# VectorE reads a unit's values before the expert sum, the next unit's maximum and the GRU's products

## What is computed

```python
x = x + attn(lstm(x, cond, Wx, Wh, b), Wq, Wkv_down, Wk_up, Wv_up, Wout)
x = x + moe(gru(x, cond, Wz, bz, Wr, br, Wh, bh, Wp, bp), gate_w, w1, b1, w2, b2)

# lstm, for each of 128 steps
a = xW[t] + h @ Wh;  i, f, o = sigmoid(a[:, :384]);  g = tanh(a[:, 384:])
c = f * c + i * g;   h = o * tanh(c)
# attn: 16 heads of 64, keys and values from a latent of 32, causal, softmax over 128 keys
# gru, for each of 128 steps
z = sigmoid([x_t, h] @ Wz + bz);  r = sigmoid([x_t, h] @ Wr + br)
h_new = (1 - z) * h + z * tanh([x_t, r * h] @ Wh + bh)
h = tanh(h_new @ Wp + bp) if (t + 1) % 4 == 0 and t < 127 else h_new
# moe: 8 experts 128 -> 512 -> 128 with gelu, the best 2 of a softmax gate
```

## Time and profile before

| | |
|---|---|
| median of 3 runs | 856.5 us (852.35 to 860.57) |
| profiled execution, its own time | 853.5 us |
| its span | 851.6 us |
| mean granted TensorE clock | 0.836 of full |
| busy: TensorE, VectorE, ScalarE, GpSimd | 80%, 47%, 42%, 15% |

### The profile page before, as it was taken

One profiled execution on the slowest core, in us unless ns is written; L12 is line 12 of the kernel. 1 busy time (PEld: TensorE's weight loads), 2 busy tenths in 40 slices (PEclk: granted clock), 3 DMA queues, 4 the chain that ended last, 5 costly groups with the idle time before them and its releaser, 6 DMA issues.

```text
span 851.6 us, 19294 instructions
## 1 busy us (share of the span) xinstructions
PE 679.1 (80%) x7090; PEld 603.3 (71%) x7090; DVE 398.2 (47%) x2308; ACT 354.2 (42%) x1240; POOL 131.5 (15%) x339
## 2 busy tenths in 40 slices
PE   6968978877788777887788778887888787788888
PEld 3536756777678667776777677776877677777787
DVE  2454553443644455445554455545555444434332
ACT  1434323343533454335533564334533563343333
POOL 3033022100420022101220032101220032000000
PEclk8886966665667998789977998789977998599999
DMA  9100000000000000000000000000000000000000
GB/s 292 76 1 2 2 1 1 2 1 1 2 1 2 4 2 2 2 7 2 2 1 1 8 2 2 1 8 2 1 2 1 8 1 1 1 8 1 1 8 10
DMA packets 5531, 10.07 MB, mean 12 GB/s; under 512 B 1827, under 2 KB 4527, under 8 KB 5054
## 3 DMA queue, kind: packets, MB, share of 16 engines
q1 hardware_dynamic: 4686, 6.47, 2.1%
q10 hardware_dynamic: 752, 2.37, 1.1%
HBM read 7.79 MB, written 1.05 MB: 10 GB/s over the span
## 4 chain that ended last, share of the span: by engine, by line
PE 63%; DVE 16%; ACT 13%; issue 6%; DMA 1%; SPq 0%; POOL 0%; DVEq 0%; POOLq 0%; ACTq 0%
PE pY L443 16%; PE pH L443 13%; PE pG L443 9%; PE pV L538 7%; PE pV L443 6%; ACT hid L798 5%; PE pL L443 5%; PE pC L443 5%; PE pS L443 4%; DVE gB L1010 2%; DVE On L919 2%; ACT L798 2%; ACT gC L810 2%; DVE ghi L1013 2%; DVE glo L1016 2%
## 5 line engine op out<-in xcount | busy, mean ns | idle before, releaser
L443 PE MATMUL pY<-w,hid 128*128 128x128 f32 x1024 | 161.2, 311 | 0.0
L443 PEld LDWEIGHTS pY<-w,hid 128*128 128x128 f32 x1024 | 146.5, 220 | 2.3
L417 POOL COPY qbd<-qh 32x256 f16<-32x256 f16 x256 | 101.5, 396 | 196.0 <-PE pS L443 180.0
L1001 DVE SCALAR_TENSOR_TENSOR gRZ<-gT,g 128x32 f32<-128x32 f32 x128 | 25.9, 203 | 199.9 <-ACT gT L805 199.4
L798 ACT ACTIVATE hid<-pH,b 128x256 f32<-128x256 f32 (+1 forms) x288 | 111.9, 445 | 12.0 <-PE pH L443 11.8
L538 PE MATMUL pV<-ident,P 128*128 128x128 f32 x256 | 59.8, 378 | 68.1 <-DVE On L919 66.4
L443 PE MATMUL pH<-ghi,w1hi 128*128 128x256 f16 (+1 forms) x288 | 77.1, 273 | 43.5 <-ACT hid L798 42.7
L805 ACT ACTIVATE gT<-pG 128x32 f32<-128x32 f32 x128 | 25.2, 197 | 187.0 <-PE pG L443 186.9
L538 PEld LDWEIGHTS pV<-ident,P 128*128 128x128 f32 x256 | 39.1, 190 | 71.9 <-ACT P L781 59.4
L443 PE MATMUL pH<-ghi,w1lo 128*128 128x256 f16 (+1 forms) x288 | 78.0, 276 | 0.0
L443 PE MATMUL pH<-glo,w1hi 128*128 128x256 f16 (+1 forms) x288 | 77.9, 276 | 0.0
(11 more groups left out here) (156 smaller groups left out, 1558.9 us busy)
## 6 DMA issues: line engine op xcount, KB each, us to landing
w<-in_w SPq DMA_DIRECT2D x2, 2048.0 KB, 10.7
out<-acc SPq DMA_DIRECT2D x16, 64.0 KB, 1.5
xT<-in_xT ACTq DMA_DIRECT2D x1, 960.0 KB, 9.6
hid<-in_WqT ACTq DMA_DIRECT2D x1, 512.0 KB, 5.4
hid<-in_Wout ACTq DMA_DIRECT2D x1, 512.0 KB, 7.6
lWh<-in_lWh SPq DMA_DIRECT2D x1, 256.0 KB, 2.7
lWx<-in_lWx SPq DMA_DIRECT2D x1, 256.0 KB, 9.2
gWh<-in_gWh SPq DMA_DIRECT2D x1, 192.0 KB, 7.1
```

Of the source, the lines that this page charges most:

```text
L417: pool.tensor_copy(qbd[r, n % 2, :, :, q, :], qh[r, p % 2, :, 2 * u:2 * u + 2, :, :].rearrange("p l b (g c) t -> p l (b g) (c t)", g=2)).t ...
L443: return nc.tensor.matmul(o, lhsT=lhsT, rhs=rhs, start=start, stop=stop, skip_group_check=True)
L1001: V.scalar_tensor_tensor(gRZ[:, :, :], gT[:, :, :], 1.0, g8[:, at:last + 1:last - at, :], ALU.add, ALU.mult).then_inc(g_rh, 1)
```

## The change

In VectorE's loop the call of `normalise` for the step's unit moves from behind the GRU's products to a place right behind `gRZ` and `gA`. The instructions, their operands and their semaphores stay the same, and so do the other engines' programs.

```diff
@@ -1001,6 +1001,8 @@
                     V.scalar_tensor_tensor(gRZ[:, :, :], gT[:, :, :], 1.0, g8[:, at:last + 1:last - at, :],
                                            ALU.add, ALU.mult).then_inc(g_rh, 1)
                     V.scalar_tensor_tensor(gA[:, :], gT[:, 1, :], -1.0, prev, ALU.add, ALU.mult).then_inc(g_a, 1)
+                if unit_at(k, O_V) is not None:
+                    normalise(unit_at(k, O_V))
                 if (k - 1, "B") in DOWN_AT and k - 1 < TAIL:
                     combine(DOWN_AT[(k - 1, "B")])
                 if unit_at(k - 1, O_S) is not None:
@@ -1014,8 +1016,6 @@
                     V.scalar_tensor_tensor(g8[:, g, :], gA[:, :], keep, gB[:, :], ALU.mult, ALU.add).then_inc(g_h, 1)
                     dve.wait_ge(g_h, g + 1)
                     V.tensor_tensor(glo[:, g, :], g8[:, g, :], ghi[:, g, :], ALU.subtract).then_inc(g_lo, 1)
-                if unit_at(k, O_V) is not None:
-                    normalise(unit_at(k, O_V))
                 if half_at(k) is not None and k % TB == O_P[1]:
                     add_x(half_at(k))
                 if t < T:
```

## The result

The changed kernel takes 765.25 us (median of 4 runs, 755.96 to 772.7), the one before in the same runs 858.54; the ratio is 0.888, with a 95% interval of 0.878 to 0.899. The forecast was 798 with a range of 778 to 822. The direction was right and the size too small: 93 us instead of 57. Medians are of all runs of a kernel, ratios leave out the runs in a slower state of the chip, so that a ratio can differ a little from the quotient of the medians.

The account below looks back on a forecast made before the run. TensorE, busy 80% of the span, was taken as the bound, with 66.4 us waiting for `On`. Gains of 53.5, less 2.0, 1.4, 1.5, 2.0, plus 10 for clock, made 56.6 off 853.5: forecast 798 us, range 778 to 822.

Parts of the forecast that it names:

- Step 1: Attention steps: reading the values earlier brings `On` forward, so TensorE's transposes wait less; 53.5 us gained, wait left 11 to 13.
- The sum: Forecast's whole-kernel total: 53.5 us gained, less 2.0, 1.4, 1.5 and 2.0, plus 10 for the clock: 56.6 us.
- Rival D: Transposes in attention steps really wait for the probabilities, so nothing happens: 855 us, chance 0.04.
- Step 2: VectorE work behind the moved pair runs later; charges 2.0, 1.4 and 1.5 us, scores' wait for P under 14.
- Rival C: VectorE, ScalarE and scores chain takes over in most steps, half the gain becomes waiting for P: 827 us, chance 0.13.
- rival E: Maximum behind the wait for the values lengthens all 64 steps by 0.7 us: slower, 898 us, chance 0.04.
- the ring: Attention step's dependency loop: values release `rs` and `On`, then maximum, exponentials, scores and next values; 0.7 us more per step if longest.
- Step 3: First attention block: maximum now follows `On`, right before the exponentials, making steps some 0.3 us longer; 2 us charged.
- Step 4: TensorE's clock in attention blocks: partly recovers, slices at 7 to 9 tenths; 10 us gained.
- the bound: Upper limit of the clock's gain in attention blocks, everything at full clock: 24 us, with 0 as lower limit.
- a floor of 4.7 to 5.1 us a step: Shortest attention step at full clock: 2.4 to 2.8 us to the last exponential, plus 2.3 from scores to next `lT`.
- Rival A: TensorE's clock comes back altogether in attention slices, all at 9 tenths or more: 783 us, chance 0.18.

## Why the prediction fell short, step by step

**Step 1, `On` comes earlier: right.** (The stretch 421:469.5 of the earlier trace rows, which I called block 4, is block 5; the two are alike, 9.1 us each.) The sum had 53.5 us; the wait fell by 66.4 - 10.9 = 55.5. The single wait in the step of rows 3 was to be 0.20 and is 0.19. Rival D, that the transposes wait for the probabilities, falls with it. Why the row of the weight loads named P was not looked into; a release by ScalarE's exponentials, which run at that time, is my guess.

**Step 2, what is queued behind: right in kind, 10.6 us instead of 4.9.** The scores' wait rose from 7.4 to 18.0; I had said under 14. The sum had charged only steps 4 and 5 because it used the slack that the low clock gives. At full clock TensorE reaches the scores earlier, and in block 4 they wait in steps 5, 6 and 7 (0.51, 0.22, 0.46). Rival C, over 30 us, did not come, nor did rival E, a loss of 45 us: the ring of maximum, exponentials and scores is now about as long as TensorE's own work, and is felt in 26 waits of 18.0 us in all, not in all 64 steps.

**Step 3, the first block: wrong in sign, by chance.** I charged 2 us. In the changed kernel the eight steps there (20 to 27) take 29.7 us instead of 32.7, because the clock is full. The stretch of the changed kernel:

```profile
69.10:98.83 29.73, 25.52 (x318) 20.73 (x317) 17.65 (x90) 14.28 (x55) 5.44 (x14) 1.00 0.01 2
```

the same steps of the kernel with zeros in the wait, whose program up to there is that of the kernel before:

```profile
68.88:98.48 29.60, 25.27 (x313) 20.73 (x317) 18.14 (x89) 14.30 (x55) 5.46 (x14) 1.00 0.01 2
```

and the kernel before itself:

```profile
69.93:102.62 32.69, 29.41 (x317) 23.12 (x317) 18.15 (x89) 14.25 (x54) 5.43 (x14) 0.84 0.01 2
```

The old order has the full clock there in one run and 0.84 in another, so the 3 us are not the change's; the changed kernel itself had the lower clock in its second profiled run (0.78 over steps 0 to 28, against 0.88). At equal clock its own cost is 0.1 us, not 2: the scores wait 0.40 there, against 0.38 in the earlier trace rows.

**Step 4, the clock: the step that failed.** The sum had 10 us with a bound of 24. What it was: of the span's 87.4 us, 55.5 are the wait, less 10.6 for the scores, so 42.5 remain for the clock and whatever else is small. TensorE's busy time, with the same records, says nearly the same: it fell by 679.1 - 634.4 = 44.7. The experiment that fills the wait and leaves it late gives 36 for the clock without any of the wait's own gain. Three things made the term too small.

- I took less than half of the bound, 10 of 24, because the row nearest to the new step was the present one, in which the clock falls. But the present step has the wait and the new one has not. The bound was about right where I had worked it out: 11 for each of blocks 3 to 7, 55 together, and they gained 54.8, although not all of them at full clock. The experiments with zeros show that filling this wait lifts the clock (0.88 to 0.96 in those blocks, against 0.74 to 0.89 with the same zeros behind).
- The bound rested on a floor of 4.7 to 5.1 us a step, which hid part of what a full clock gives. The step above takes 4.42: the last exponential ends 312.71 - 310.57 = 2.14 behind `lT`, not 2.4, and the next `lT` follows the scores after 2.13, not 2.3, since that 2.3 was read from a step that ran partly at 1.2 GHz. Block 4, the only one at full clock, gained 14.9 us where the bound allowed 11; block 3, whose clock stayed low, gained 5.4.
- For block 2 and what lies beside it I had put 8 us together with block 8. There the clock was lowest, and up to step 51 the kernel gained 20.2 us, where the sum had 7.0 for block 2's wait less 2.0 for the first block; 3.8 of the 20.2 lie in steps 0 to 28 and are the chance of step 3. I had read from the earlier trace rows that slices without attention have 9 tenths or more; steps 43 to 51 have no unit's transposes that wait, and 0.57. They gained 5.5 us, which no term of the sum held. The eight steps from 36 on became 11.4 us shorter, where the wait explains at most 8.4. Before:

```profile
136.14:187.88 51.74, 41.80 (x408) 36.77 (x409) 23.09 (x148) 18.70 (x75) 6.17 (x16) 0.66 0.00 1
```

and after:

```profile
132.30:172.60 40.30, 36.52 (x409) 32.08 (x409) 22.45 (x146) 17.75 (x75) 6.07 (x16) 0.80 0.01 1
```

Rival A, the clock comes back altogether, was nearest, but it is not what happened either: the clock came back in part (0.836 to 0.899), and that part gave more than the 24 us that A has for all of it, so its 783 was still 18 too high.

What stays open is how much of the 42.5 us comes by the length of the single wait and how much by TensorE's idle time in all; half of the units moved gave 49 us, of which 31 are the wait's, but its profile does not show a higher clock in the blocks. Open is also why the clock of the same program differs from one execution to the next by as much as in block 3 (0.66 and 0.95).

## What to carry to other kernels

Ask of every result that another engine waits for where it stands in its own engine's queue: two short operations (0.46 us) behind six that nobody was in a hurry for held TensorE for 66 us. Where TensorE's clock moves between its levels, price a wait of TensorE twice, once for its length and once for what its end may give back through the clock; here the second was over half of the first. Look at the clock stretch by stretch and in more than one execution before a gain or a cause is read from it. And read a floor for the new time from a step that already ran at the clock that is expected.

## What the hardware showed that was not expected

Idle times of mostly 1.2 to 1.4 us, one in each step of 6 to 7 us, went together with TensorE at 1.2 GHz for some 40% of an attention block (clock 0.79). 36 groups of useless products put into these waits made the kernel 36 us faster, with a clock of 0.88 to 0.96 in the six blocks; the same groups one place later in the queue made it 14.5 us slower, with 0.74 to 0.89 there. And the clock is not a property of the program alone: the same block of the same kernel had 0.66 in one execution and 0.95 in another.
